# Block-diagonal queries and values placed by SBUF-to-SBUF transfers instead of ScalarE and GpSimd

## What is computed

```python
x = x + _L0_xattn_ref(_layernorm(x), ctx_4096, ctx_4096)      # autocorrelation, top 9 delays
x = x + _L0_ffn_ref(_layernorm(x), ...)                       # base matmul + 2 of 8 low-rank experts
x = x + _L1_xattn_ref(_layernorm(x), ctx_4096, Wq, bq, ...)   # the layer that the change touches
x = x + _L1_ffn_ref(_layernorm(x), ...)                       # 2 of 4 low-rank experts
...
def _L1_xattn_ref(x, cond, ...):          # 8 heads of 16 channels, a window of 16 positions
    q = _pointwise(Wq, bq, x); k = _pointwise(Wk, bk, cond); v = _pointwise(Wv, bv, cond)
    ...
    dots = jnp.einsum('bhdt,bhdtw->bhtw', qh, k_win) * scale
    attn = jax.nn.softmax(dots, axis=-1)
    out = jnp.einsum('bhtw,bhdtw->bhdt', attn, v_win)
```

## Time and profile before

| | |
|---|---|
| median of three runs | 1869.83 us (1869.39 to 1873.03) |
| span of the profiled execution | 1871.1 us |
| TensorE busy / VectorE / ScalarE / GpSimd | 92% / 84% / 73% / 55% of the span |
| period of one step in the middle | 55.2 us |
| all transfers | 77.82 MB, mean 42 GB/s |
| mean granted clock of TensorE | 0.973 |

### The profile page before, as it was taken

The page is one execution under the profiler, slowest core; times in us unless marked ns, Lnnn a source line. Parts: engine busy times, 40 slices in busy tenths (PEclk is TensorE's granted clock), DMA queues, the critical chain, the costliest instruction groups (busy, mean ns, idle before and its releaser), DMA issues. The chain is left out here.

```text
span 1871.1 us, 48299 instructions
## 1 busy us (share of the span) xinstructions
PE 1712.3 (92%) x19296; PEld 1078.5 (58%) x19296; DVE 1575.8 (84%) x4726; ACT 1372.6 (73%) x2121; POOL 1028.3 (55%) x934
## 2 busy tenths in 40 slices
PE   3689999999999999999999999999999999999875
PEld 1355566666556656556666655666665566565543
DVE  5778898888888888889888888988888888888853
ACT  4277777878777787877777887778787777878753
POOL 1555556556555656655556655555565556566542
PEclk7899999999999999999999999999999999999995
DMA  5111110111010111101011110101110101111000
GB/s 208 34 35 36 35 46 25 47 46 46 24 47 27 44 46 47 47 24 47 24 47 46 47 38 33 46 25 47 46 46 24 47 28 43 46 47 35 2 12 24
DMA packets 20977, 77.82 MB, mean 42 GB/s; under 512 B 2704, under 2 KB 2960, under 8 KB 20240
## 3 DMA queue, kind: packets, MB, share of 16 engines
q1 hardware_dynamic: 20752, 74.72, 11.7%
HBM read 57.94 MB, written 16.78 MB: 40 GB/s over the span
## 5 line engine op out<-in xcount | busy, mean ns | idle before, releaser
L586 PE MATMUL pb<-w_base_h,even_words 128*128 128x512 f16 x1024 | 324.8, 379 | 0.0
L1438 POOL TENSOR_TENSOR p_hl<-sc,p_hl 128x512 f16<-128x512 f32 x128 | 164.2, 1283 | 206.6 <-ACT p_hl L764 206.6
L877 ACT ACTIVATE q_diag<-sc,par 32x512 f32<-32x512 f32 x384 | 269.4, 717 | 8.0
L1483 POOL TENSOR_TENSOR sc<-sc,sc_rec 128x512 f32<-128x512 f32 x128 | 134.4, 1050 | 216.8 <-DVE sc_rec L1245 216.6
L586 PE MATMUL pb<-w_base_l,even_words 128*128 128x512 f16 x512 | 193.9, 379 | 0.0
L473 PE MATMUL pa<-xn_a,tab 128*128 128x512 f32 x384 | 180.5, 606 | 4.6 <-ACT xn_a L764 4.6
L660 PEld LDWEIGHTS pc<-sc_t,v_diag 128*128 128x128 f16 x6144 | 170.2, 97 | 20.6 <-DVE sc_t L1252 6.0
L660 PE MATMUL pc<-sc_t,v_diag 128*128 128x32 f16 x6144 | 173.9, 177 | 5.6 <-DVE sc_t L1252 5.6
L637 PE MATMUL pc<-k_h,q_diag 128*128 128x32 f16 x2048 | 169.1, 177 | 0.0
L638 PE MATMUL pc<-k_l,q_diag 128*128 128x32 f16 x2048 | 168.4, 177 | 0.0
L639 PE MATMUL pc<-k_h,q_diag 128*128 128x32 f16 x2048 | 168.4, 177 | 0.0
(11 more groups left out here) (170 smaller groups left out, 5008.1 us busy)
## 6 DMA issues: line engine op xcount, KB each, us to landing
x_a<-in_x SPq DMA_DIRECT2D x32, 512.0 KB, 3.6
x_res<-in_ctx_in SPq DMA_DIRECT2D x32, 512.0 KB, 4.4
x_res<-in_x SPq DMA_DIRECT2D x32, 512.0 KB, 4.5
out<-rows_c SPq DMA_DIRECT2D x32, 512.0 KB, 2.9
v_diag<-in_base_w SPq DMA_DIRECT2D x4, 1024.0 KB, 10.4
q_diag<-in_ra SPq DMA_DIRECT2D x1, 544.0 KB, 14.1
q_diag<-in_b SPq DMA_DIRECT2D x1, 512.0 KB, 15.8
q_diag<-in_b SPq DMA_DIRECT2D x2, 256.0 KB, 17.0
```

Of the source, the lines that this page charges most:

```text
L586: mm(pb[:, h, :], rows[:, cols], weights[:, j, h * HALF:(h + 1) * HALF], start=(j == 0 and m == 0), stop=False)
L877: nc.scalar.activation(q_diag[rows, blocks, col:col + QB], source, ACT.Copy, scale=par[rows, a:a + 1]).then_inc(qd_out.sem, 1)
L1438: g_.tensor_tensor(part[:, :, :, LO], sc[:, g % 2, :, :], part[:, :, :, HI], ALU.subtract)\
L1483: g_.tensor_tensor(sc[:, g % 2, :, :], sc[:, g % 2, :, :], sc_rec[:, blocks].unsqueeze(2).to_broadcast([P, GB, KEYS]), ALU.mult)\
```

## The change

The activations and GpSimd instructions that fill `q_diag` and `v_diag` are gone. SyncE issues transfers from `v_t` and `q_hl` to the same places. For a sequence these are 4 + 4 transfers for values (32 partitions x 64 pieces) and 8 for queries (one per head, 16 partitions x 64 pieces). A piece is 16 f32, 64 bytes. `v_diag` is laid out with even and odd blocks apart, so that a transfer's destination is one regular pattern. TensorE waits once for all queries and once for all values. The store goes to the end of SyncE's step.

```diff
-        v_diag = sb("v_diag", [P, NBLK, 2, P // 2])
+        v_diag = sb("v_diag", [P, 2, NBLK // 2, 2, P // 2])
...
+            def place_values(b, odd):
+                sp.wait_ge(vt_out.sem, vt_out.after(b, odd + 1))
+                if odd == 0:
+                    sp.wait_ge(vdiag_set.sem, 1)
+                    if not first(b):
+                        sp.wait_ge(mm_av.sem, mm_av.after(b - 1))
+                for pair in range(PAIRS):
+                    rows = slice(32 * pair, 32 * pair + 32)
+                    place = v_diag[rows, odd, :, :, pair * HD:(pair + 1) * HD].rearrange("p m a d -> p (m a) d")
+                    sp.dma_start(place, v_t[odd][rows, :].rearrange("p (n d) -> p n d", d=HD))\
+                        .then_inc(v_placed.sem, 16)
+
+            def place_queries(b):
+                sp.wait_ge(ql_out.sem, ql_out.after(b))
...
+                for head in range(HEADS):
+                    rows = slice(HD * head, HD * (head + 1))
+                    sp.dma_start(q_diag[rows, :, rows], q_hl[rows, :].rearrange("p (n t) -> p n t", t=QB))\
+                        .then_inc(q_placed.sem, 16)
...
                 if live(1):
                     load_x_res(i - 1)
-                if live(3):
-                    store(i - 3)
+                if live(2):
+                    place_values(i - 2, 0)
+                if live(-1) and not first(i):
+                    load_x(i + 1)
+                if live(2):
+                    place_values(i - 2, 1)
+                    place_queries(i - 2)
                 if live(-1):
                     load_ctx(i + 1)
-                if live(-2):
-                    load_x(i + 2)
+                if live(3):
+                    store(i - 3)
...
-                if g % 2 == 0:
-                    pe.wait_ge(qd_out.sem, qd_out.after(b, (g // 2 + 1) * 2 * (PAIRS - 1)))
-                    pe.wait_ge(qd_pool.sem, qd_pool.after(b, (g // 2 + 1) * 2))
                 if g == 0:
+                    pe.wait_ge(q_placed.sem, q_placed.after(b))
...
                 if g == 0:
-                    pe.wait_ge(vd_out.sem, vd_out.after(b))
-                    pe.wait_ge(vd_pool.sem, vd_pool.after(b))
+                    pe.wait_ge(v_placed.sem, v_placed.after(b))
```

More of the change, by code:

```diff
@@ L350, in build @@
         PAIRS = HEADS // 2
[L351 to L355, removed]
+        v_placed = signal("v_placed", 16 * 2 * PAIRS)
+        q_placed = signal("q_placed", 16 * HEADS)
         mm_sc = signal("mm_sc", NG)
@@ L431, in store @@
                 sp.dma_start(out[b], rows_c[:, :]).then_inc(out_done.sem, 16)
+            def place_values(b, odd):
[11 more added lines that the diff above has]
+                sp.wait_ge(ql_out.sem, ql_out.after(b))
+                sp.wait_ge(qdiag_set.sem, 1)
+                if not first(b):
+                    sp.wait_ge(mm_sc.sem, mm_sc.after(b - 1))
+                for head in range(HEADS):
+                    rows = slice(HD * head, HD * (head + 1))
+                    sp.dma_start(q_diag[rows, :, rows], q_hl[rows, :].rearrange("p (n t) -> p n t", t=QB))\
+                        .then_inc(q_placed.sem, 16)
             load_x(0)
@@ L659, in c_attend @@
                     for m, (v_part, p_part) in enumerate(((HI, HI), (HI, LO), (LO, HI))):
-                        last = mm(place, v_halves[:, blk, :, v_part], p_halves[:, g % 2, i, :, p_part],
+                        last = mm(place, v_halves[:, blk % 2 * NBLK // 2 + blk // 2, :, v_part], p_halves[:, g % 2, i, :, p_part],
                                   start=(m == 0), stop=(m == 2))
@@ L843, in b_values @@
                                      bias=bias_att[:, 2:3]).then_inc(vh_out.sem, 1)
[L845 to L857, removed]
             def b_queries(b):
@@ L864, in b_queries @@
                     .then_inc(qh_out.sem, 1)
[L866 to L878, removed]
             def experts_exp(b, n, source, experts):
@@ L900, in c_high @@
                 if g == 0:
-                    act.wait_ge(vd_out.sem, vd_out.after(b))
+                    act.wait_ge(v_placed.sem, v_placed.after(b))
                 act.wait_ge(p_out.sem, p_out.after(b, g + 1))
@@ L1233, in c_subtract @@
                 if g == 1:
-                    dve.wait_ge(qd_out.sem, qd_out.after(b))
-                    dve.wait_ge(qd_pool.sem, qd_pool.after(b))
+                    dve.wait_ge(q_placed.sem, q_placed.after(b))
                 v.tensor_tensor(sc[:, g % 2, :, :], source,
@@ L1445, in a_normalise @@
                     .then_inc(prob_out.sem, 1)
-            pool_rows = slice(32 * POOL_PAIR, 32 * POOL_PAIR + 32)
-            def b_value_blocks(b, odd):
-                if first(b) and odd == 0:
-                    pool.wait_ge(vdiag_set.sem, 1)
-                pool.wait_ge(vt_out.sem, vt_out.after(b, odd + 1))
-                if odd == 0:
-                    if not first(b):
-                        pool.wait_ge(mm_av.sem, mm_av.after(b - 1))
-                place = v_diag[pool_rows, :, :, POOL_PAIR * HD:(POOL_PAIR + 1) * HD]\
-                    .rearrange("p (m o) a d -> p o m a d", o=2)[:, odd]
-                g_.tensor_tensor(place, v_t[odd][pool_rows, :].rearrange("p (m a d) -> p m a d", a=2, d=HD),
-                                 one[pool_rows, :].unsqueeze(2).unsqueeze(3).to_broadcast([32, NBLK // 2, 2, HD]),
-                                 ALU.mult).then_inc(vd_pool.sem, 1)
-                pool.wait_ge(vd_pool.sem, vd_pool.after(b, odd + 1))
-            def b_query_blocks(b, a, half):
-                if first(b) and a == 0 and half == 0:
-                    pool.wait_ge(qdiag_set.sem, 1)
-                if a == 0:
-                    pool.wait_ge(ql_out.sem, ql_out.after(b))
-                    if not first(b):
-                        pool.wait_ge(mm_sc.sem, mm_sc.after(b - 1, 2 * half + 2))
-                col = (2 * POOL_PAIR + a) * QB
-                blocks = slice(half * NBLK // 2, (half + 1) * NBLK // 2)
-                g_.tensor_tensor(q_diag[pool_rows, blocks, col:col + QB],
-                                 q_hl[pool_rows, :].rearrange("p (n t) -> p n t", t=QB)[:, blocks],
-                                 par[pool_rows, a:a + 1].unsqueeze(2).to_broadcast([32, NBLK // 2, QB]),
-                                 ALU.mult).then_inc(qd_pool.sem, 1)
-                pool.wait_ge(qd_pool.sem, qd_pool.after(b, 2 * half + a + 1))
             def c_normalise(b, g):
```

44 lines of the change are left out of this document (6 added, 38 removed).

## The result

The changed kernel takes 2228.94 us (median of 4, 2223.9 to 2234.82) against 1869.83 of the kernel before: a ratio of 1.191, 95% interval 1.189 to 1.194. A fourth execution of the kernel before took 2011.45 us, in a slow state of the chip, and is not counted. The changed kernel is 359.1 us slower, 11.22 us in each of 32 steps. The forecast was 2135 with a range of 1855 to 2825. The direction and the place of the stall came true; the size was 266 us where 359 were measured, because the pieces moved more slowly than was predicted.

A forecast was written before the change was run, and what follows sets the result against it. TensorE, busy 92%, was taken to bound the kernel. Per step 6.7 (stall) + 2.0 (clock) - 0.4 (VectorE) = 8.3 us, 266 us over 32 steps, gave a median of 2135 us; range 1855 to 2825.

The forecast's parts named there:

- No slack for the queries, nothing hides the stall: TensorE's first scores: queries were ready just in time, so their lateness stalls TensorE 6.7 us in each of 32 steps.
- The price of a piece: Each 64-byte piece inside SBUF takes 12 ns on a DMA engine, bounds 5 and 27 ns, estimated from nearest packets.
- Moving: Odd values and queries in SyncE's queue: 1024 pieces per engine at 12 ns, 12.3 us from 940.45 on.
- The fixed part: Time from issue to signal that is neither issuing of others nor moving: 1.6 us, added once after the moving.
- Issuing: SyncE issues the 12 transfers of odd values and queries 0.43 us apart, 4.7 us, less than the moving.
- under 0.5 was named as a sign: SyncE held for less than 0.5 us by each issue, the last queries transfer landing 8 to 10 us after issue.
- The clock: TensorE after a stall of over 5 us: lower granted clock loses 2.0 us a step, lower bound 0.
- The gain: VectorE no longer waits for a square root behind GpSimd's fillings: 0.4 us a step, at most 2.63.
- Rival 1: Pieces overlap at 5 ns or less, so TensorE starts the first scores about as before: 1855 to 1874 us; chance 0.13.
- Rival 2: A 64-byte piece costs 27 ns, like one of 512 bytes: 29.8 us more a step, 2825 us; chance 0.20.
- Rival 3: SyncE's issue time is per row: 6.9 us a values transfer, 3.4 a queries one; near 4050 us; chance 0.13.
- the stall's term: TensorE ahead of the first scores: start at 954.3 instead of 947.62, waiting for all queries, 6.7 us a step.

The follow-up runs named there:

- the filler run: The changed kernel with TensorE repeating the mask matmul 40 times ahead of its wait for the queries; 2188.76 us, 40 us less than the changed kernel.

## Why the prediction was right, and where it was off

- **No slack for the queries, nothing hides the stall:** right. The wait ahead of L653 is 10.2 of the 11.22 us, and moving the values out of its way takes 5.2 us off it.
- **The price of a piece, 12 ns:** right as the duration of a packet. The queue's packet time went from 0.117 x 16 x 1871.1 = 3503 to 0.344 x 16 x 2222.1 = 12,230 us, 8727 us for 786,432 pieces: 11.1 ns, with the signals' packets counted in. The number of pieces was right to the last one (the queue has 815,376 - 20,752 = 794,624 packets more, which are 786,432 pieces and 16 further packets for each of 512 new transfers). Halving the pieces gave 12.0 ns. But a duration is not the time from one piece to the next.
- **Moving, 1024 x 12 ns = 12.3 us:** this is the term that was mis-sized. It took the recorded duration of a packet for the pace. The pieces moved for 16.2 us, and in the 7 us of queries one came every 15.3 ns on an engine though it was recorded with 11.5: the DMA engines were idle for a quarter of that stretch. Two runs show what the duration leaves out. Spread over all partitions, the same transfers and pieces moved in 12.4 us; and in 16 partitions each further transfer cost 0.33 us beyond its pieces. How these two hang together is open.
- **The fixed part, 1.6 us:** nearly right. From the first issue to the first piece are 1.2 us and from the last piece to TensorE's start 0.6, together 1.8. With 16.2 of moving these are 18.0 us against 13.9, 4.1 more in the step shown, of which 3.5 show in the mean wait (10.2 against 6.7).
- **Issuing, 4.7 us:** wrong, but not a term of the sum, which took the larger of issuing and moving. SyncE was held for 15.0 us by the twelve issues, 1.0 us each for queries and 1.7 for values, where under 0.5 was named as a sign; and the queries landed 4.3 us after their issue, not 8 to 10. Most of the waiting work stood in SyncE, not in the queue behind it.
- **The clock, 2.0 us:** the sign and the place were right, the size 1.26 us (the filler run).
- **The gain, 0.4 us:** 10.2 + 1.26 - 11.22 leaves 0.2, and the wait at L532 fell from 0.52 to 0.15. That agrees, but 0.2 is a remainder, no more exact than the terms it is left by; where the gain could be seen by itself, with the values alone moved, it did not come, since ScalarE's query fillings stood in its place.
- **Rival 1 (hidden):** the pace would have had to be 5.4 ns a piece; it was 15.3. Fell.
- **Rival 2 (27 ns a piece):** fell for its reason. A piece of 64 bytes has 11.1 ns, one of 512 has 27. The rule of 512 bytes in the Trainium skill ("DMA: Bandwidth & Descriptors", Specifications) does not show here as a dearer small packet. The rival's doubt about transfers that reach few rows of SBUF held: a third of the wait.
- **Rival 3 (SyncE makes the pieces):** an issue lasts 1.0 us for queries and 1.7 for values, not 3.4 and 6.9. With two queues the hold of an odd-value transfer grows from 1.7 to 3.0 us, with the same pieces to make, which speaks for back pressure and against making. Fell.

In sum, 8.3 us a step were predicted as 6.7 + 2.0 - 0.4, and 11.22 came as 10.2 + 1.26 - 0.2. The clock's term was 0.7 too high and hid a part of the 3.5 that the stall's term was too low.

## What to carry to other kernels

Before work is moved from an engine to a queue of transfers, ask when its result is needed, not how full the engine is. Here the values' transfers, two thirds of the pieces, cost nothing, and with half of the queries' the kernel became 1% faster, because these are needed some 15 us after they are made. With the other half too, which is needed after 6 us, it was 19% slower with the odd values ahead of the queries and 11% with the queries first. A queue works in order, so what is needed first goes first; and what is put last has somebody waiting for it, too. Count for a transfer of small pieces the pieces, the transfers and the partitions that it reaches, and do not take the duration of a packet for the pace.

## What the runs showed of the hardware

- A 64-byte piece inside SBUF is recorded with about 11 ns (9.6 to 11.5 in the stretches shown). On each of 16 engines one comes every 15.3 ns if a transfer has 16 partitions and 1024 pieces, every 12.3 ns with 32 partitions and 2048 pieces, every 11.7 ns with 128 partitions and 1024 pieces. In 16 partitions a further transfer adds about 0.33 us.
- The issuer is held while pieces wait: by 1.0 us for a transfer of 1024 pieces, by 1.4 to 1.7 for one of 2048, by 3.0 if a second queue is at work; a load of 128 rows held it for 0.33 us. How much a queue takes before it holds the issuer was not measured.
- In an idle stretch of 10.7 us TensorE's granted clock fell to 0.50, its level of 1.2 GHz, and the kernel became 40 us faster by 1,280 matmuls of no use in it.
